# A gated recurrence on one core: each gate of each half in a PSUM bank of its own and turned by itself

## The chip, the cores and the metric

One core of one Trainium2 chip. The metric is the device time of one launch in microseconds; three runs of the kernel before took 1808.76, 1807.4 and 1808.27, median 1808.27.

## The reference

x has shape (8, 512, 512): 8 sequences (B) of 512 steps (T) of 512 features. Weights and state are float32.

```
def step(h, x_t):
    fused = sigmoid(concat([x_t, h]) @ w_W + w_b)
    r, z = split(fused, 2)
    memory = x_t @ wx_W + wx_b + r * (h @ wh_W + wh_b)
    h_new = z * h + (1 - z) * tanh(memory)
    return h_new, h_new
out = x + all h_new
```

In the kernel r is the gate of the first half of `fused`, m the memory part, z the second half of `fused`. The 512 steps depend on each other through h.

## The kernel before, in words

The 512 features of h are four chunks of 128 (KC = 4), in two halves: A holds chunks 0 and 1, B chunks 2 and 3. For each step TensorE computes h @ [w_r, w_m, w_z] with h as the loaded weights (8 columns, the batch) and the weight matrix moving. Each product is split over four column tiles of 32 (`tile_position=(0, Q * j)`, j = 0 to 3), so the instructions go out in fours. A float32 matmul stands in the trace as two weight loads and two matmuls.

`products(group, half, s)` (line 226) makes the part of one group that comes from one half of h. The groups are RM_A (r and m of half A, 128 columns, bank 0), RM_B (bank 1), Z_A (64 columns, bank 2), Z_B (bank 3). `step` on TensorE (line 237): wait for half A of h, RM_A and RM_B of that half; wait for half B of h, RM_A, Z_A both halves, RM_B, wait until Z_B of the step before has been turned, Z_B both halves. Then `x_products` (line 214) makes 3 of the 48 chunk products of x for the block of 16 steps that comes next, from weights and x that SP loads anew (`wx_step`, `x_next`), into banks 4 to 6. TensorE's loop holds four steps, the other engines' 16.

VectorE turns a group (`turn`, line 322): a 32 by 32 block transpose from PSUM into `turned`, after which the features lie on partitions. Then it adds the x part (`sum_r` line 327, `sum_z` line 331), forms r * hm + xm in a scan (`mix_m`, line 335), and z * h - z * n + n in a scan (`mix_h`, line 343), which gives h. ScalarE makes the sigmoids (`reset` line 275, `update` line 279) and the tanh (`new` line 283), empties the x products (`empty`, line 264) and places them (`place_x`, line 271). GpSimd adds the bias to m (`hidden`, line 401) and x to the output (`add_x`, line 407).

The order on each engine is written out by hand in its `step` function (lines 237, 289, 351, 420). All waits are on counting semaphores. A wait is written ahead of the instruction it guards; where there are several, one rides on the instruction and the others are instructions of their own on the engine's queue. Each half of h has its semaphore `h_ready`, each group `..._done` (TensorE finished) and `..._turned` (VectorE finished).

Of the kernel before, what the change touches and what calls it, by code (L numbers as in the profile page):

```python
# [12 lines left out]
def build(nc, x, h0, w_h, w_x, b_x, b_h, out):  # L13
# [40 lines left out]
    with ctx:  # L54
# [30 lines left out]
        ps = ctx.enter_context(nc.psum_tensor("ps", [P, 8, 512], F32))  # L85
        X_BANK = 4

# [25 lines left out]

        rm_a_done = sem("rm_a_done")
        z_a_done = sem("z_a_done")
        rm_b_done = sem("rm_b_done")
        z_b_done = sem("z_b_done")
        rm_a_turned = sem("rm_a_turned")
        z_a_turned = sem("z_a_turned")
        rm_b_turned = sem("rm_b_turned")  # L120
        z_b_turned = sem("z_b_turned")
        x_product = sem("x_product")
# [9 lines left out]
        hm_ready = halves("hm_ready")  # L132
        xg_ready = sem("xg_ready")
        xg_turned = sem("xg_turned")
# [10 lines left out]
        def _(sp):  # L145
# [18 lines left out]

            for r in range(RING):
                load_wx(r)
                sp.dma_start(x_next[:, r], x_flat[:, :, TOK:2 * TOK]).then_inc(x_next_loaded[r], 16)  # L167
            sp.dma_start(x_sb[:, :, TOK:2 * TOK], x_flat[:, :, TOK:2 * TOK]).then_inc(x_loaded, 16)
            with sp.Fori(0, BLOCKS) as i:
# [4 lines left out]
                for s in range(STEPS):  # L174
                    if s % RING == 0:
                        turn = sp.snap(i * (STEPS // RING) + (s // RING + 1))
                    if s % RING < RING - 1:
                        sp.wait_ge(x_used[s % RING], turn)
                    else:
                        sp.wait_ge(x_product, sp.snap(i * UNITS + (s // RING + 1) * X_UNITS + UNITS))  # L180
                    load_wx((s + RING) % STEPS)
                    if s >= STEPS - RING:
                        sp.dma_start(x_next[:, s % RING], x_flat[:, :, cols]).then_inc(x_next_loaded[s % RING], 16)
                sp.wait_ge(y_added, sp.snap(i * STEPS + 2 * STEPS))
# [11 lines left out]
        def _(pe):  # L196
            def x_product_of(u, k, w, moving):
                for j in range(TILES):
                    at = slice(Q * j, Q * (j + 1))
                    mm = pe.matmul(ps[at, X_BANK + u % X_UNITS, 0:TOK], w[:, at], moving,  # L200
                                   start=(k == 0), stop=(k == KC - 1), tile_position=(0, Q * j))
                if k == KC - 1:
                    mm.then_inc(x_product, 1)
                return mm

            def first_x_products():
                for u, k in x_list:
                    if k == 0 and u >= X_UNITS:
                        pe.wait_ge(xg_ready, u - X_UNITS + 1)
# [4 lines left out]
            def x_products(i, s):  # L214
# [11 lines left out]
            def products(group, half, s):  # L226


                at, cols, bank = group
                for k in range(half * HC, (half + 1) * HC):  # L230
                    for j in range(TILES):
                        mm = pe.matmul(ps[Q * j:Q * j + B, bank, 0:cols], h_of(s - 1, k),  # L232
                                       wh[:, k, j, at:at + cols], start=(k == 0), stop=(k == KC - 1),
                                       tile_position=(0, Q * j))
                return mm

            def step(t0, s):
# [12 lines left out]

            pe.wait_ge(x0_loaded, 16)
            first_x_products()
# [3 lines left out]
            with nc.Fori(0, T // RING, engines=(mybir.EngineType.PE,), hint_back_edge=True) as i:  # L256
                t0 = pe.snap(i * RING)
                for s in range(RING):
                    step(t0, s)
                    x_products(i, s)  # L260

        @block.scalar
        def _(act):
            def empty(u, which, unit0):
                act.wait_ge(bias_loaded, 2 * 16)
                act.wait_ge(x_product, unit0 + (u + 1))
                dst = xg[:, which, :, u, :].rearrange("p a t b -> p (a t) b")
                act.activation(dst, ps[:, X_BANK + u % X_UNITS, 0:TOK].rearrange("p (t b) -> p t b", b=B),  # L268
                               ACT.Identity, bias=bias_x[:, u:u + 1]).then_inc(xg_ready, 1)

# [17 lines left out]

            def step(t0, s, this, other, unit0):
                nxt = held(act, t0 + (s + 1))  # L290
                reset(0, nxt)
                update(0, nxt)
                new(0, s, nxt)
                reset(1, nxt)
                update(1, nxt)
                new(1, s, nxt)
                for u in X_ENDS[s]:
# [3 lines left out]
                else:  # L301
                    act.wait_ge(xg_ready, unit0 + UNITS)
                    act.sem_inc(xg_turned, 1)
                    place_x(other, 0)
# [3 lines left out]
            for u in range(UNITS):  # L308
                empty(u, slice(0, 1), 0)
            act.wait_ge(xg_ready, UNITS)  # L310
            place_x(slice(0, 1), 0)
            with nc.Fori(0, BLOCKS, engines=(mybir.EngineType.Activation,), hint_back_edge=True) as i:
# [4 lines left out]
                for s in range(STEPS):  # L317
                    step(t0, s, this, other, unit0)

        @block.vector  # L320
        def _(dve):
            def turn(bank, o, g0, g1):
                cols = (g1 - g0) * HC * Q
                return dve.transpose(turned[:, o, g0:g1].rearrange("p g c q -> p (g c) q"),  # L324
                                     ps[:, bank, 0:cols].rearrange("p (c q) -> p c q", q=Q))

# [23 lines left out]

            def step(t0, i, s):
# [24 lines left out]
                mix_h(1, s, nxt)  # L376

            dve.sem_inc(z_b_turned, 1)
            dve.memset(ps[:, 0:GROUP_BANKS, :], 0.0).then_inc(ps_cleared, 1)  # L379
# [14 lines left out]
            with nc.Fori(0, BLOCKS, engines=(mybir.EngineType.DVE,), hint_back_edge=True) as i:  # L394
                t0 = dve.snap(i * STEPS)
                for s in range(STEPS):
                    step(t0, i, s)

        @block.gpsimd
        def _(pool):  # L400
            def hidden(o, par, nxt):
                pool.wait_ge(rm_b_turned if o else rm_a_turned, nxt)
                pool.tensor_tensor(add[:, par, o, M, :, 0].rearrange("p (c b) -> p c b", b=B), product_of(o, M),  # L403
# [79 lines left out]
```

## Time and profile before

| | |
|---|---|
| median of the runs | 1808.27 us |
| the profiled execution: its own time / span | 1807.97 / 1806.1 us |
| granted TensorE clock | 0.998 |
| TensorE busy, weight loads busy | 1787.5 us (99%), 1629.9 us (90%) |
| VectorE, ScalarE, GpSimd busy | 1160.5 us (64%), 824.9 us (46%), 357.1 us (20%) |
| instructions on TensorE | 78208 matmuls, 78208 weight loads |
| DMA engines, mean busy share of the one hardware queue | 29.6% |
| weights `wx_step`: issue to landing | 2.4 us, 516 transfers of 192 KB |
| `x_next`: issue to landing | 3.2 us, 132 transfers of 256 KB |

Busy times are sums of the recorded durations; a matmul's end is modelled and matmuls overlap. PEld is the weight load of TensorE, DVE is VectorE, ACT ScalarE, POOL GpSimd, SP the queue that issues the DMAs. "idle before" is the time in which the engine stood still just before the instructions of a group, with what ended it.

### The profile page before, as it was taken

Reading aid. Unit: us, or ns where it says so; the run is one execution under the profiler, and the core shown is the slowest. Engines: PE = TensorE matmul, PEld = TensorE weight load, DVE = VectorE, ACT = ScalarE, POOL = GpSimd, SP = SyncE. Lnnn points to the kernel's source line nnn. Section 1 sums busy time; section 2 is a strip of 40 time slices with the busy share of each in tenths; the row PEclk is TensorE's granted clock in tenths of the full one; section 3 lists DMA queues with packets and bytes.
Section 4 is the critical chain, followed back from the end, with each engine's and each line's share of the span. In section 5 each row is a group of like instructions: output and inputs, shape, how many; then the busy total and the mean of one; then the engine's idle time right before and its main releaser. Section 6 shows DMA issues by size and latency. Waiting matters only on the chain.

```text
span 1806.1 us, 178513 instructions
## 1 busy us (share of the span) xinstructions
PE 1787.5 (99%) x78208; PEld 1629.9 (90%) x78208; DVE 1160.5 (64%) x6153; ACT 824.9 (46%) x3983; POOL 357.1 (20%) x1540
## 2 busy tenths in 40 slices
PE   7999999999999999999999999999999999999998
PEld 6999999999999999999999999999999999999997
DVE  2666666666666666666666666666666666666665
ACT  2444444444444444444444444444444444444444
POOL 0222222222222222222222222222222222222221
PEclk9999999999999999999999999999999999999999
DMA  6222333223332223332233322233322333223332
GB/s 218 87 67 86 91 91 91 73 75 91 91 91 85 69 86 92 92 92 69 81 92 92 91 77 74 88 91 91 91 68 80 91 91 92 74 74 94 92 92 82
DMA packets 180731, 159.86 MB, mean 89 GB/s; under 512 B 12016, under 2 KB 179440, under 8 KB 180720
## 3 DMA queue, kind: packets, MB, share of 16 engines
q1 hardware_dynamic: 180720, 159.72, 29.6%
q8 instruction: 7, 0.11, 0.0%
q14 instruction: 4, 0.03, 0.0%
HBM read 151.28 MB, written 8.39 MB: 88 GB/s over the span
## 4 chain that ended last, share of the span: by engine, by line
PE 98%; SPq 1%; DMA 0%; issue 0%; DVE 0%; ACT 0%; POOL 0%; POOLq 0%; DVEq 0%
PE ps L232 78%; PE ps L200 20%; SPq L167 0%; SPq L162 0%; DMA x_sb<-in_x 0%; SPq L153 0%; SPq L159 0%; DVE turned L324 0%; SPq L150 0%; DVE h L347 0%; DVE m_pre L338 0%; SPq L157 0%; SPq L156 0%; SPq L155 0%; DVE pre_r L328 0%
## 5 line engine op out<-in xcount | busy, mean ns | idle before, releaser
L232 PE MATMUL ps<-wh,h 128*8 128x128 f32 (+1 forms) x65536 | 1504.7, 246 | 2.6 <-issue 2.2
L232 PEld LDWEIGHTS ps<-wh,h 128*8 128x8 f32 x65536 | 1324.7, 90 | 143.1 <-DVE h L347 113.5
L324 DVE STREAM_TRANSPOSE turned<-ps 128x128 f32<-128x128 f32 (+1 forms) x2048 | 550.4, 269 | 412.4 <-PE ps L232 412.4
L277 ACT ACTIVATE m_by<-pre_r 128x16 f32<-128x16 f32 x1024 | 224.2, 219 | 701.2 <-DVE pre_r L328 701.2
L200 PE MATMUL ps<-x_next,wx_step 128*32 128x128 f32 x12288 | 433.0, 274 | 0.6 <-issue 0.6
L347 DVE TENSOR_TENSOR_SCAN h<-h_by,h 128x48 f32<-128x48 f32 x1024 | 274.2, 268 | 152.4 <-ACT h L286 152.4
L403 POOL TENSOR_TENSOR add<-turned,bias_h 128x16 f32<-128x16 f32 x1024 | 222.8, 218 | 709.9 <-DVE turned L324 681.5
L281 ACT ACTIVATE h_by<-pre_z 128x16 f32<-128x16 f32 x1024 | 229.6, 224 | 249.8 <-DVE pre_z L332 246.0
L200 PEld LDWEIGHTS ps<-x_next,wx_step 128*32 128x32 f32 x12288 | 316.1, 110 | 16.2 <-issue 4.3
L416 POOL TENSOR_TENSOR y<-x_sb,h 128x32 f32 x512 | 134.0, 262 | 734.5 <-DVE h L347 734.5
L286 ACT ACTIVATE h<-m_pre 128x32 f32<-128x32 f32 x1024 | 237.8, 232 | 1.8 <-DVE m_pre L338 1.8
L338 DVE TENSOR_TENSOR_SCAN m_pre<-m_by,add 128x32 f32<-128x32 f32 x1024 | 223.2, 218 | 1.8 <-POOL add L403 1.8
L332 DVE TENSOR_TENSOR pre_z<-turned,add 128x16 f32<-128x16 f32 x1024 | 180.3, 176 | 35.0
L328 DVE TENSOR_TENSOR pre_r<-turned,add 128x16 f32<-128x16 f32 x1024 | 179.8, 176 | 34.9
L268 ACT ACTIVATE xg<-ps,bias_x 128x128 f32 (+1 forms) x396 | 145.6, 368 | 15.0 <-PE ps L200 14.9
L273 ACT ACTIVATE add<-xg 128x96 f32 (+1 forms) x513 | 145.6, 284 | 3.9
L200 PE MATMUL ps<-x_sb,wx 128*32 128x128 f32 x384 | 15.1, 323 | 9.8 <-DMA wx<-in_w_x 6.1
L200 PEld LDWEIGHTS ps<-x_sb,wx 128*32 128x32 f32 x384 | 13.3, 131 | 11.0 <-issue 10.3
L379 DVE MEMSET ps<- 128x2048 f32 x1 | 1.8, 1765 | 1.3 <-PEq L475 1.3
L391 DVE COPY h<-h 128x8 f32<-128x8 f32 x4 | 0.4, 170 | 2.9 <-DMA h<-in_h 2.9
L307 ACT ACTIVATE warm<-bias_h 128x4 f32<-128x4 f32 x1 | 0.2, 205 | 4.3 <-DMA bias_h<-in_b_h 4.3
L307 ACT ACT_TABLE_LOAD x1 | 1.3, 1283 | 0.7 <-PEq L475 0.7
(8 smaller groups left out, 1.1 us busy)
## 6 DMA issues: line engine op xcount, KB each, us to landing
wx_step<-in_w_x SPq DMA_DIRECT2D x516, 192.0 KB, 2.4
x_next<-in_x SPq DMA_DIRECT2D x132, 256.0 KB, 3.2
x_sb<-in_x SPq DMA_DIRECT2D x34, 256.0 KB, 3.2
out_h<-y SPq DMA_DIRECT2D x32, 256.0 KB, 2.9
wx<-in_w_x SPq DMA_DIRECT2D x6, 512.0 KB, 7.3
wh<-in_w_h SPq DMA_DIRECT2D x4, 768.0 KB, 11.0
bias_x<-in_b_x SPq DMA_DIRECT2D x1, 6.0 KB, 3.2
bias_h<-in_b_h SPq DMA_DIRECT2D x1, 2.0 KB, 3.6
```

The source lines that it names most:

```text
L200: mm = pe.matmul(ps[at, X_BANK + u % X_UNITS, 0:TOK], w[:, at], moving, start=(k == 0), stop=(k == KC - 1), tile_position=(0, Q * j))
L232: mm = pe.matmul(ps[Q * j:Q * j + B, bank, 0:cols], h_of(s - 1, k), wh[:, k, j, at:at + cols], start=(k == 0), stop=(k == KC - 1), tile_po ...
L268: act.activation(dst, ps[:, X_BANK + u % X_UNITS, 0:TOK].rearrange("p (t b) -> p t b", b=B), ACT.Identity, bias=bias_x[:, u:u + 1]).then_i ...
L277: act.activation(m_by[:, o, :, 1], pre_r[:, o, :], ACT.Sigmoid).then_inc(r_ready[o], 1)
L281: act.activation(h_by[:, o, :, 2], pre_z[:, o, :], ACT.Sigmoid).then_inc(z_ready[o], 1)
L286: act.activation(n_twice, m_pre[:, o, :, 1].unsqueeze(2).to_broadcast([P, HB, 2]), ACT.Tanh)\
L324: return dve.transpose(turned[:, o, g0:g1].rearrange("p g c q -> p (g c) q"), ps[:, bank, 0:cols].rearrange("p (c q) -> p c q", q=Q))
L328: dve.tensor_tensor(pre_r[:, o].rearrange("p (c b) -> p c b", b=B), product_of(o, R), x_of(par, o, R), ALU.add).then_inc(r_summed[o], 1)
L332: dve.tensor_tensor(pre_z[:, o].rearrange("p (c b) -> p c b", b=B), product_of(o, Z), x_of(par, o, Z), ALU.add).then_inc(z_summed[o], 1)
L338: dve.tensor_tensor_scan(m_pre[:, o].rearrange("p i w -> p (i w)"), m_by[:, o].rearrange("p i w -> p (i w)"), add[:, par, o, M].rearrange( ...
L347: dve.tensor_tensor_scan(h[:, s % RING, o, 0:REGION], h_by[:, o].rearrange("p i w -> p (i w)"), h[:, (s - 1) % RING, o, 1:1 + REGION], 0.0 ...
L403: pool.tensor_tensor(add[:, par, o, M, :, 0].rearrange("p (c b) -> p c b", b=B), product_of(o, M), bias_h[:, HC * o:HC * (o + 1)].unsqueez ...
```

## The change

- Six groups instead of four: r, m and z of each half, 64 columns each, in banks 0 to 5 (`GATES * o + g`); the host lays the columns of w_h out to match. Each has its own `done` and `turned` semaphore and its own turn on VectorE: six turns of 64 columns per step instead of two of 128 and two of 64.
- TensorE's order: half A of h for r0, m0, z0 and m1; wait for half B of h; r0, m0, z0 (second half), r1 whole, m1 (second half), z1 whole. The wait for Z_B's turn is gone.
- VectorE's order: turn r0, turn m0, sum r0, turn z0, turn r1, sum z0, mix_m 0, turn m1, sum r1, mix_h 0, turn z1, mix_m 1, sum z1, mix_h 1.
- ScalarE's order: the tanh of half B comes ahead of the sigmoid of its z.
- The x products use banks 6, 7, 6 for units 0, 1, 2, with a semaphore for each of the three in place of one. TensorE no longer waits for `x_next`: SP waits for it before it issues the weights. The values TensorE waits for are computed once per loop pass, between the groups.
- At the start SP issues the four `x_next` loads first, then waits for each before its `wx_step` load.

```
-    RM_A = (0, P, 0)
-    RM_B = (P, P, 1)
-    Z_A = (2 * P, P // 2, 2)
-    Z_B = (2 * P + P // 2, P // 2, 3)
-    GROUP_BANKS = 4
+    GROUP = HC * Q
+    GROUP_BANKS = HALVES * GATES
+    X_BANKS = [GROUP_BANKS, GROUP_BANKS + 1, GROUP_BANKS]
...
@@ sync: start, and steps 12 to 15 of a block
             for r in range(RING):
+                sp.dma_start(x_next[:, r], x_flat[:, :, TOK:2 * TOK]).then_inc(x_next_loaded[r], 16)
+            for r in range(RING):
+                sp.wait_ge(x_next_loaded[r], 16)
                 load_wx(r)
-                sp.dma_start(x_next[:, r], x_flat[:, :, TOK:2 * TOK]).then_inc(x_next_loaded[r], 16)
...
+                    if s >= STEPS - RING:
+                        sp.dma_start(x_next[:, s % RING], x_flat[:, :, cols]).then_inc(x_next_loaded[s % RING], 16)
+                        sp.wait_ge(x_next_loaded[s % RING], sp.snap(i * 16 + 32))
                     load_wx((s + RING) % STEPS)
...
@@ tensor: x products
-                pe.wait_ge(wx_step_loaded[s], held(pe, i * 16 + 16))
-                pe.wait_ge(x_next_loaded[s], held(pe, (i // (STEPS // RING)) * 16 + 16))
+                pe.wait_ge(wx_step_loaded[s], loaded)
...
-                        pe.wait_ge(xg_ready, held(pe, i * X_UNITS + (UNITS - X_UNITS + u + 1)))
+                        if u == 0:
+                            pe.wait_ge(xg_free[2], free)
+                        elif u == 1:
+                            pe.wait_ge(xg_free[1], free)
+                        else:
+                            pe.wait_ge(xg_free[0], again)
...
@@ tensor: one step
                 pe.wait_ge(h_ready[0], nxt)
-                products(RM_A, 0, s)
-                products(RM_B, 0, s)
+                products(0, R, 0, s, True)
+                products(0, M, 0, s, True)
+                products(0, Z, 0, s, True)
+                products(1, M, 0, s, True)
                 pe.wait_ge(h_ready[1], nxt)
-                products(RM_A, 1, s).then_inc(rm_a_done, 1)
-                products(Z_A, 0, s)
-                products(Z_A, 1, s).then_inc(z_a_done, 1)
-                products(RM_B, 1, s).then_inc(rm_b_done, 1)
-                pe.wait_ge(z_b_turned, nxt)
-                products(Z_B, 0, s)
-                products(Z_B, 1, s).then_inc(z_b_done, 1)
+                products(0, R, 1, s, False).then_inc(r_done[0], 1)
+                products(0, M, 1, s, False).then_inc(m_done[0], 1)
+                products(0, Z, 1, s, False).then_inc(z_done[0], 1)
+                products(1, R, 0, s, True)
+                products(1, R, 1, s, False).then_inc(r_done[1], 1)
+                products(1, M, 1, s, False).then_inc(m_done[1], 1)
+                products(1, Z, 0, s, True)
+                products(1, Z, 1, s, False).then_inc(z_done[1], 1)
...
@@ scalar: one step
                 reset(1, nxt)
+                new(1, s, nxt)
                 update(1, nxt)
-                new(1, s, nxt)
...
@@ vector: one step
+                dve.wait_ge(r_done[0], nxt)
                 if s % RING == 0:
                     dve.wait_ge(y_added, held(dve, t0 + (s + STEPS)))
-                dve.wait_ge(rm_a_done, nxt)
-                turn(0, 0, R, Z).then_inc(rm_a_turned, 1)
-                dve.wait_ge(rm_a_turned, nxt)
+                turn(0, R).then_inc(r_turned[0], 1)
+                dve.wait_ge(m_done[0], nxt)
+                turn(0, M).then_inc(m_turned[0], 1)
                 dve.wait_ge(x_placed, nxt)
+                dve.wait_ge(r_turned[0], nxt)
                 sum_r(0, par, nxt)
-                dve.wait_ge(z_a_done, nxt)
-                turn(2, 0, Z, GATES).then_inc(z_a_turned, 1)
-                dve.wait_ge(z_a_turned, nxt)
+                dve.wait_ge(z_done[0], nxt)
+                turn(0, Z).then_inc(z_turned[0], 1)
+                dve.wait_ge(r_done[1], nxt)
+                turn(1, R).then_inc(r_turned[1], 1)
+                dve.wait_ge(z_turned[0], nxt)
                 sum_z(0, par, nxt)
                 mix_m(0, par, nxt)
-                dve.wait_ge(rm_b_done, nxt)
-                turn(1, 1, R, Z).then_inc(rm_b_turned, 1)
-                dve.wait_ge(rm_b_turned, nxt)
+                dve.wait_ge(m_done[1], nxt)
+                turn(1, M).then_inc(m_turned[1], 1)
+                dve.wait_ge(r_turned[1], nxt)
                 sum_r(1, par, nxt)
                 mix_h(0, s, nxt)
-                dve.wait_ge(z_b_done, nxt)
-                turn(3, 1, Z, GATES).then_inc(z_b_turned, 1)
-                dve.wait_ge(z_b_turned, held(dve, t0 + (s + 2)))
+                dve.wait_ge(z_done[1], nxt)
+                turn(1, Z).then_inc(z_turned[1], 1)
+                mix_m(1, par, nxt)
+                dve.wait_ge(z_turned[1], nxt)
                 sum_z(1, par, nxt)
-                mix_m(1, par, nxt)
                 mix_h(1, s, nxt)
```

## Rows read from the trace of the kernel before

**Rows 1.** The page: chain that ended last by engine; the queue that fetches code

```profile
PE 98%; SPq 1%; DMA 0%; issue 0%; DVE 0%; ACT 0%; POOL 0%; POOLq 0%; DVEq 0%
...
q8 instruction: 7, 0.11, 0.0%
```

**Rows 2.** Groups of instructions, 300 to 1700 us: busy us, mean ns | idle before <-releasers

```profile
L232 PEld LDWEIGHTS ps<-wh,h 128*8 128x8 f32 x51824 | 1046.9, 90 | 110.1 <-DVE h L347 89.4
L232 PE MATMUL ps<-wh,h 128*8 128x128 f32 x25908 | 901.5, 273 | 0.0
L232 PE MATMUL ps<-wh,h 128*8 128x64 f32 x25920 | 510.4, 219 | 0.0
...
L200 PEld LDWEIGHTS ps<-x_next,wx_step 128*32 128x32 f32 x9720 | 249.8, 110 | 12.1 <-issue 3.2
...
L324 DVE STREAM_TRANSPOSE turned<-ps 128x64 f32<-128x64 f32 x810 | 188.9, 233 | 0.0
```

**Rows 3.** Chain of waits, 912 to 920 us: start us, us, what

```profile
914.45 0.66 PE ps L200 x24
```

**Rows 4.** Timeline of one step: start us, us, engine line op out<-in xcount [idle <-releaser]

```profile
912.49 0.34 PEld L232 LDWEIGHTS ps<-wh,h 128*8 128x8 f32 x16 [0.24 <-DVE h L347]
913.19 0.32 DVE L324 STREAM_TRANSPOSE turned<-ps 128x128 f32<-128x128 f32 x1 [0.75 <-PE ps L232]
...
913.64 0.25 DVE L324 STREAM_TRANSPOSE turned<-ps 128x64 f32<-128x64 f32 x1
...
913.92 0.18 DVE L332 TENSOR_TENSOR pre_z<-turned,add 128x16 f32<-128x16 f32 x1
914.01 0.22 DVE L338 TENSOR_TENSOR_SCAN m_pre<-m_by,add 128x32 f32<-128x32 f32 x1
...
914.15 0.29 DVE L324 STREAM_TRANSPOSE turned<-ps 128x128 f32<-128x128 f32 x1
...
914.47 0.18 DVE L328 TENSOR_TENSOR pre_r<-turned,add 128x16 f32<-128x16 f32 x1
...
914.57 0.28 DVE L347 TENSOR_TENSOR_SCAN h<-h_by,h 128x48 f32<-128x48 f32 x1
...
914.77 0.22 DVE L324 STREAM_TRANSPOSE turned<-ps 128x64 f32<-128x64 f32 x1
...
915.02 0.17 DVE L332 TENSOR_TENSOR pre_z<-turned,add 128x16 f32<-128x16 f32 x1
915.11 0.22 DVE L338 TENSOR_TENSOR_SCAN m_pre<-m_by,add 128x32 f32<-128x32 f32 x1
...
915.23 0.22 ACT L281 ACTIVATE h_by<-pre_z 128x16 f32<-128x16 f32 x1 [0.33 <-DVE pre_z L332]
915.36 0.23 ACT L286 ACTIVATE h<-m_pre 128x32 f32<-128x32 f32 x1
...
915.63 0.26 DVE L347 TENSOR_TENSOR_SCAN h<-h_by,h 128x48 f32<-128x48 f32 x1 [0.30 <-ACT h L286]
...
915.94 0.23 PEld L232 LDWEIGHTS ps<-wh,h 128*8 128x8 f32 x12 [0.22 <-DVE h L347]
```

**Rows 5.** Timeline, start of a step with s = 0 mod 4 (PEld, DVE)

```profile
902.10 1.22 PEld L232 LDWEIGHTS ps<-wh,h 128*8 128x8 f32 x64 [0.21 <-DVE h L347]
...
902.87 0.32 DVE L324 STREAM_TRANSPOSE turned<-ps 128x128 f32<-128x128 f32 x1 [0.82 <-PE ps L232]
```

**Rows 6.** Line 356, whole run: ns min/median/max, first and last start us

```profile
L356 DVEq EVENT_SEMAPHORE  x96: 21/21/21, 44.9 to 1788.2; - x96
```

**Rows 7.** Waits of the DMA queue, 800 to 1000 us: total us, times, longest us

```profile
SPq L162 <- PE ps L200: 157.7, 54, 3.2
```

**Rows 8.** Timeline of PE in the loop's first pass, first and last of four

```profile
32.25 1.24 PE L232 MATMUL ps<-wh,h 128*8 128x64 f32 x60 [0.28 <-issue]
...
42.71 0.63 PE L200 MATMUL ps<-x_next,wx_step 128*32 128x128 f32 x11 [0.59 <-issue]
```

**Rows 9.** DMA queues, 0 to 60 us: packets, MB, share of 16 engines

```profile
q8 instruction: 7, 0.11, 0.8%
```

More of the change, by code:

```diff
@@ L132, in build @@
         hm_ready = halves("hm_ready")
-        xg_ready = sem("xg_ready")
+        xg_free = [sem(f"xg_free{u}") for u in range(X_UNITS)]
         xg_turned = sem("xg_turned")
@@ L207, in first_x_products @@
                 for u, k in x_list:
-                    if k == 0 and u >= X_UNITS:
-                        pe.wait_ge(xg_ready, u - X_UNITS + 1)
+                    if k == 0 and u >= X_UNITS - 1:
+                        last = max(v for v in range(u) if X_BANKS[v % X_UNITS] == X_BANKS[u % X_UNITS])
+                        pe.wait_ge(xg_free[last % X_UNITS], last // X_UNITS + 1)
                     if k == 0 and u * WX_PARTS % UNITS == 0:
@@ L212, in first_x_products, with x_products @@
                     x_product_of(u, k, wx[:, u, k, :], x_sb[:, k, 0:TOK])
-            def x_products(i, s):
-                pe.wait_ge(wx_step_loaded[s], held(pe, i * 16 + 16))
-                pe.wait_ge(x_next_loaded[s], held(pe, (i // (STEPS // RING)) * 16 + 16))
+            def x_products(loaded, free, again, s):
+                pe.wait_ge(wx_step_loaded[s], loaded)
                 for n in range(X_EACH):
@@ L224, in x_products, with products @@
                     last.then_inc(x_used[s], 1)
-            def products(group, half, s):
-                at, cols, bank = group
+            def products(o, g, half, s, start):
+                bank = GATES * o + g
+                at = GROUP * bank
                 for k in range(half * HC, (half + 1) * HC):
                     for j in range(TILES):
-                        mm = pe.matmul(ps[Q * j:Q * j + B, bank, 0:cols], h_of(s - 1, k),
-                                       wh[:, k, j, at:at + cols], start=(k == 0), stop=(k == KC - 1),
-                                       tile_position=(0, Q * j))
-                return mm
@@ L237, in step @@
-            def step(t0, s):
+                        mm = pe.matmul(ps[Q * j:Q * j + B, bank, 0:GROUP], h_of(s - 1, k),
+                                       wh[:, k, j, at:at + GROUP], start=(start and k % HC == 0),
+                                       stop=(not start and k % HC == HC - 1), tile_position=(0, Q * j))
+                return mm
+            def step(i, t0, s):
+                nonlocal loaded, free, again
                 nxt = held(pe, t0 + (s + 1))
                 pe.wait_ge(h_ready[0], nxt)
-                products(RM_A, 0, s)
-                products(RM_B, 0, s)
-                pe.wait_ge(h_ready[1], nxt)
-                products(RM_A, 1, s).then_inc(rm_a_done, 1)
-                products(Z_A, 0, s)
-                products(Z_A, 1, s).then_inc(z_a_done, 1)
-                products(RM_B, 1, s).then_inc(rm_b_done, 1)
-                pe.wait_ge(z_b_turned, nxt)
-                products(Z_B, 0, s)
-                products(Z_B, 1, s).then_inc(z_b_done, 1)
+                products(0, R, 0, s, True)
+                products(0, M, 0, s, True)
+                if s == 0:
+                    loaded = held(pe, i * 16 + 16)
+                products(0, Z, 0, s, True)
+                if s == 0:
+                    free = held(pe, i + UNITS // X_UNITS)
+                    again = held(pe, i + (UNITS // X_UNITS + 1))
+                products(1, M, 0, s, True)
+                pe.wait_ge(h_ready[1], nxt)
+                products(0, R, 1, s, False).then_inc(r_done[0], 1)
[6 more added lines that the diff above has]
+                products(1, Z, 1, s, False).then_inc(z_done[1], 1)
@@ L251, in _ @@
+            loaded = free = again = None
             pe.wait_ge(x0_loaded, 16)
@@ L258, in _ @@
                 for s in range(RING):
-                    step(t0, s)
-                    x_products(i, s)
+                    step(i, t0, s)
+                    x_products(loaded, free, again, s)
         @block.scalar
@@ L287, in new, with step @@
                     .then_inc(tanh_ready[o], 1)
-            def step(t0, s, this, other, unit0):
+            def step(i, t0, s, this, other, unit0):
                 nxt = held(act, t0 + (s + 1))
@@ L301, in step @@
                 else:
-                    act.wait_ge(xg_ready, unit0 + UNITS)
-                    act.sem_inc(xg_turned, 1)
+                    for p in range(X_UNITS):
+                        act.wait_ge(xg_free[p], held(act, i * (UNITS // X_UNITS) + 2 * (UNITS // X_UNITS)))
+                        act.sem_inc(xg_turned, 1)
                     place_x(other, 0)
@@ L309, in _ @@
                 empty(u, slice(0, 1), 0)
-            act.wait_ge(xg_ready, UNITS)
+            for p in range(X_UNITS):
+                act.wait_ge(xg_free[p], UNITS // X_UNITS)
             place_x(slice(0, 1), 0)
@@ L317, in _, with turn @@
                 for s in range(STEPS):
-                    step(t0, s, this, other, unit0)
+                    step(i, t0, s, this, other, unit0)
         @block.vector
         def _(dve):
[L322 to L325, printed above, removed]
+            def turn(o, g):
+                return dve.transpose(turned[:, o, g], ps[:, GATES * o + g, 0:GROUP].rearrange("p (c q) -> p c q", q=Q))
             def sum_r(o, par, nxt):
@@ L396, in _ @@
                 for s in range(STEPS):
-                    step(t0, i, s)
+                    step(t0, s)
         @block.gpsimd
@@ L462 @@
     to_h = rows_h.reshape(P, KC, 3, J, 2, KC // 2, Q).transpose(0, 1, 3, 2, 4, 5, 6)
[L463 to L464 removed]
+    h_cols = to_h.transpose(0, 1, 2, 4, 3, 5, 6).reshape(P, KC, J, 3 * P)
     arrays = {
```

30 lines of the change are left out of this document (12 added, 18 removed).

## The prediction

> **What bounds the kernel now.** I read the chain of waits first, and it misleads a little: it puts 98% of the span on TensorE [rows 1]. TensorE's ends are modelled and overlap, so "busy" does not say whether work or a wait sets a step. The groups of instructions over 1400 us do. 810 transposes of half a step's z are 405 steps, so a step takes 1400/405 = 3.457 us, and 512 steps are 1770 us of the profiled 1806.1 us span [rows 2]. The matmuls go out in fours, one for each column tile of 32. The 24 of an x product stage take 0.66 us [rows 3], so a four of 128 columns takes 0.110 us. A 64-column matmul is 273 - 219 = 54 ns shorter, so its four takes 0.056 us. A step has 22 fours of 128 (16 of r and m, 6 of x) and 16 of 64 (z). That makes 22 x 0.109 + 16 x 0.056 = 3.29 us of pure streaming (0.109 closes better than 0.110 over the step). So TensorE has a hole of 0.16 us in each step. The weight loads show where: they idle before a load that VectorE's h scan releases, 89.4 us over those 405 steps, 0.22 us each, most of it this hole [rows 2]. The kernel is bound by the recurrence, from one second-half h to the next, and not by TensorE's work.
>
> The timeline of one step shows that loop [rows 4]. In hundredths of a us, from the weight load that waits for the second half of h (912.49): turn of half A's r and m at 0.70, turn of half A's z at 1.15, pre_z 1.43, m_pre 1.52, turn of half B's r and m 1.66, pre_r 1.98, h scan of half A 2.08, turn of half B's z 2.28, pre_z 2.53, m_pre 2.62, tanh 2.87, h scan of half B 3.14, next load 3.45. From the first z turn on every item starts as soon as the one before lets it. Each turn that had to wait for TensorE starts 0.26 after its last four has streamed: 4 x 0.109 = 0.44 gives 0.70, and 8 x 0.056 more gives 1.15.
>
> **The change, part by part.** (1) r and m in groups of 64 columns: 16 fours of 0.109 become 32 of 0.056, +0.04 us of TensorE work per step. A step of pure work is then 48 x 0.056 + 0.66 + 0.01 = 3.36 us, still under 3.457, so this lies in the hole and costs nothing by itself.
>
> (2) The new loop. Times t count from that same weight load. VectorE's program now has turn r0, turn m0, sum r0, turn z0, then turn r1, and only behind it sum z0. Half A's r, m, z take 12 fours and half B's r 8: r1 is complete at 20 x 0.056 = 1.12, plus 0.26: turn r1 starts at t = 1.38. Turn z0 could be summed at about 0.97 + 0.28 = 1.25, yet sum z0 stands behind turn r1. No row shows an independent instruction behind a turn. The others let the next one in about 0.08 before their recorded end: sum 0.18 long, next after 0.09; m_pre 0.22 long, next after 0.14; h scan 0.28 long, next after 0.20 [rows 4]. So I take 0.25 - 0.08 = 0.17 for a turn that waited (z at 913.64), and 0.22 - 0.08 = 0.14 for one that did not (914.77). The bounds are 0.09 (a sum's) and the whole turn with its signal, 0.28 and 0.25. Then: sum z0 1.55, m_pre 1.64, tanh +0.25 = 1.89, h scan A +0.27 (tanh to scan in the old tail, 915.36 to 915.63) = 2.16. Turn m1 and sum r1 fit before it (1.64 + 0.14 + 0.14 + 0.09 = 2.01). Turn z1 is at 2.16 + 0.20 = 2.36, against 2.28 before: 0.08 later.
>
> (3) The tail. m_pre of half B no longer waits for the z turn: 2.36 + 0.14 = 2.50, tanh 2.75. ScalarE's order is now tanh before the z sigmoid. The sigmoid goes in 0.14 behind the tanh (that spacing: 915.23 to 915.36), at 2.89, which is later than sum z1 allows (2.63 + 0.21). It is ready 0.22 + 0.03 later, at 3.14. So the h scan now waits last for z and no longer for tanh.
>
> (4) What that wait costs. Where an instruction waits for two semaphores, the first named rides on it and the second is an instruction of its own ahead. One step in four shows its price when it is the last to come. There the turn of r and m also waits for y, and TensorE's signal is taken by such a separate wait (96 of them, line 356). The turn starts at 902.87 - 902.10 = 0.77 and not at 0.70 [rows 4 to 6]. So 0.07 is paid when the separate one comes last. mix_h names tanh first and z second, hence z rides separately: scan B at 3.14 + 0.07 = 3.21. Bounds 0 and 0.09. From scan to load 0.31 as now: 3.52.
>
> (5) The same rule takes the y wait out of the way in that one step in four (0.07/4 = 0.02 per step, now in the 3.457): its separate wait is now y's, long past. The turn, r0, would be off the path in any case.
>
> (6) Fewer waits at x products, no wait for half B's turned z, a separate semaphore for each bank: TensorE has some 0.16 us spare in each new step (3.52 - 3.36), so shorter issue there gives nothing. Before, these waits were hidden in the hole as well. The h of half A arrives at 2.16 + 0.31 = 2.47, and the x products end at 32 x 0.056 + 0.66 = 2.45. That is a stall of 0.02 to 0.05, inside the same spare.
>
> (7) SP: in steps 12 to 15 it waits for x_next to land before it issues the weights. It waits 157.7/54 = 2.9 us per step now [rows 7], and the buffers are needed three steps (over 10 us) later: nothing. At the start, x_next before wx_step moves the second x load by about a us either way: taken as 0, range 1.5 us.
>
> Sum: 3.52 unrounded is 3.515, so 3.515 - 3.457 = +0.058 us x 512 = +29.7 us. The profiled execution took 1807.97 us (span 1806.1 and 1.9 around it), 0.3 under the median of the runs, so no correction: 1837.7, forecast **1837 us**.
>
> Size of the unknowns on the loop: both turns at 0.09 and the separate wait free: 3.33, under TensorE's 3.36, so TensorE would rule. Both turns whole, and 0.05 for the first four of 64 columns after a stall (its spacing could stay that of a 128 four): 3.79.
>
> The Trainium skill, "VectorE: DVE Perf Modes", section "The DRAIN you can't avoid", says the next VectorE op does not start until the pipe is empty, and its rules ask to keep the number of ops low; that speaks against two more turns per step. The rows go against it here: sums 0.18 long are followed after 0.09 [rows 4]. By the rows the sum is the 3.52 above, by that rule it is rival C below.
>
> **Rivals.** A, faster: the tail is as short as its lower bounds and TensorE sets the step. For it: half B's z is complete on TensorE 8 fours of r and m and 16 of z (0.87 + 0.90 = 1.77, plus 0.26 = 2.03) after the load but turned at 2.28, so VectorE and not TensorE was late there; and m_pre now starts before z is turned. Against it: sum z0 behind turn r1, and the separate wait of 0.07. Step 3.36 to 3.40: -0.097 x 512 = -50, 1758 us; with 0.04 of holes -29, 1779 us. I take 1765. It decides if the loop falls under 3.40, so if the three unknowns together give back 0.12 or more.
>
> B, no change: the z signal is not paid extra (0.07 gone) and the rest stands. 3.448 against 3.457: -0.009 x 512, 1803 us, at the edge of what can be told. The loop exchanges one late item for another.
>
> C, a turn holds VectorE to its end: 0.11 more at each of turns r1 and z1, signal included, 3.74: +145, 1953 us; without the signal's share (0.08 each) 3.68, 1922 us. For it: no row shows a turn followed at once. Against it: every other op of this engine lets the next in early. This is what the drain rule of the Trainium skill, cited above, would make of the turns.
>
> D, code: TensorE's loop grows from 4 x 304 = 1216 to 4 x 432 = 1728 matmuls and weight loads. The whole run now fetches 7 packets of code [rows 1], all in its first 60 us, with four issue waits of 0.28 to 0.59 in the loop's first pass [rows 8, 9]; later passes fetch none, so the loop stays loaded. If the longer one does not, seven fetches of 0.45 per four steps cost 0.79 a step, about +400: 2210 us. The Trainium skill, "Runtime: NRT & Kernel Launch", section "Instruction fetch mechanics", gives TensorE room for 2048 instructions, which would hold 1728; the same section's remark on two cache lines would not, and the 7 packets disagree with it already for the present loop.
>
> **How the numbers follow.** Forecast 0.50 (its own range 1815 to 1865), A 0.24, B 0.14, C 0.06, D 0.06. A change of under 0.2% (1804.7 to 1811.9 us) can't be told from none; of B I count 0.05 as faster and 0.09 as the same. Faster 0.24 + 0.05 = 0.29, same 0.09, slower 0.50 + 0.06 + 0.06 = 0.62. The range 1775 to 1890 leaves out about half of A, C and D: some 0.2.
>
> **What would show it.** After: the turn of r1 starts 1.38 after the load that waits for h; sum z0 0.17 behind it; h scan of half B released last by the z sigmoid and not by tanh; step 3.51 to 3.52; the idle time of TensorE's weight loads still near 0.2 us per step, now in two places. The prediction is wrong if that idle time is near none (A), if a sum follows a turn after 0.22 or more (C), or if code packets exceed about 12 (D).

## The result, and the profile after

The changed kernel took 1795.56 us (median of 4 runs, 1794.16 to 1796.07), the kernel before 1808.51 beside it: ratio 0.9927, 95% interval 0.991 to 0.9944. It is 13 us faster; the forecast was 29 us slower. The profiled execution has a span of 1793.5 us.

Two things moved, in opposite directions. The step is the mean distance of the same signal over 360 steps of one profiled execution; the rest is the span of that execution less 512 such steps, so it holds the start of the run and also its end. Each ratio is to runs of the kernel before made beside that kernel.

| kernel | step, us | rest, us | median, us | ratio to before (95%) |
|---|---|---|---|---|
| before | 3.458 | 35.4 | 1808.51 | |
| after | 3.415 | 45.3 | 1795.56 | 0.9927 (0.991 to 0.9944) |
| e1: sum z0 ahead | 3.344 | 45.5 | 1759.73 | 0.9727 (0.971 to 0.9743) |
| e2: z rides | 3.353 | 43.2 | 1768.16 | 0.9774 (0.9758 to 0.9791) |
| e3: x early | 3.415 | 45.7 | 1795.98 | 0.9925 (0.9909 to 0.9942) |
| e4: x waits back | 3.427 | 45.7 | 1801.95 | 0.9956 (0.994 to 0.9973) |
| e5: tail back | 3.472 | 44.7 | 1824.28 | 1.0082 (1.0065 to 1.0099) |
| e6: y wait back | 3.417 | 46.0 | 1797.45 | 0.993 (0.9914 to 0.9947) |
| e7: sum waits | 3.567 | 43.9 | 1872.25 | 1.0344 (1.0327 to 1.0361) |
| b1: before, tail order | 3.468 | 36.7 | 1814.45 | 1.0025 (1.0016 to 1.0035) |
| b2: before, 64 columns | 3.469 | 44.2 | 1822.27 | 1.0068 (1.0051 to 1.0085) |
| v2: half B joined | 3.362 | 44.9 | 1766.82 | 0.9761 (0.9745 to 0.9777) |
| v3: joined, turned apart | 3.335 | 43.7 | 1753.05 | 0.9681 (0.9665 to 0.9698) |

The steps brought (3.458 - 3.415) x 512 = -22 us, the rest took 9.9 us back. The rest spreads from 43.2 to 46.0 us over the changed kernel and e1 to e7, one execution each, so a difference of 1 or 2 us in it can't be told from none. The profiled execution of e2 took 1762.96 us, 5 us under the median of its four runs (1762.96 to 1770.16): its step and rest belong to a faster execution than its median.

Of the 9.9 us, 2.7 lie at the end: from the start of the last h scan to the end of the span it is 1806.1 - 1800.98 = 5.2 us before and 1793.5 - 1785.60 = 7.9 us after. The last rows of SP and GpSimd show why, first before:

```profile
1801.52 0.26 POOL L416 TENSOR_TENSOR y<-x_sb,h 128x32 f32 x1 [1.43 <-DVE h L347]
1802.09 0.64 SPq L186 DMA_DIRECT2D out_h<-y  x1
```

then after:

```profile
1785.95 0.55 SPq L181 DMA_DIRECT2D x_next<-in_x  x1
1786.13 0.26 POOL L437 TENSOR_TENSOR y<-x_sb,h 128x32 f32 x1 [1.38 <-DVE h L365]
1789.18 0.33 SPq L158 DMA_DIRECT2D wx_step<-in_w_x  x1
1789.85 0.64 SPq L186 DMA_DIRECT2D out_h<-y  x1
```

SP now waits until x_next has landed before it issues the weights, and the last store of the output stands behind both on its queue. It is issued 3.7 us after the last addition of x starts, and 0.6 us after it in the kernel before. The same holds in all ten kernels with the new wait (3.3 to 4.0 us) and in none of the three without it (0.6 us). No run took this wait out by itself. The other 7 us lie ahead of the last h scan; b2 and e3 below show where.

The groups of the kernel after, 300 to 1700 us, beside [rows 2] (busy us, mean ns | idle before). The idle time in front of the weight loads is 54.8 us over 410 steps, 0.13 us each, where it was 0.27:

```profile
L239 PE MATMUL ps<-wh,h 128*8 128x64 f32 x78739 | 1202.5, 219 | 0.0
L239 PEld LDWEIGHTS ps<-wh,h 128*8 128x8 f32 x78729 | 1111.6, 90 | 54.8 <-DVE h L365 0.2
```

The timeline of VectorE and ScalarE after, from the turn of r1 on, which answers to [rows 4]:

```profile
916.57 0.25 DVE L343 STREAM_TRANSPOSE turned<-ps 128x64 f32<-128x64 f32 x1 [0.20 <-PE ps L239]
916.74 0.14 DVE L350 TENSOR_TENSOR pre_z<-turned,add 128x16 f32<-128x16 f32 x1
916.80 0.21 DVE L356 TENSOR_TENSOR_SCAN m_pre<-m_by,add 128x32 f32<-128x32 f32 x1
...
917.04 0.23 ACT L304 ACTIVATE h<-m_pre 128x32 f32<-128x32 f32 x1
917.07 0.14 DVE L346 TENSOR_TENSOR pre_r<-turned,add 128x16 f32<-128x16 f32 x1
...
917.31 0.26 DVE L365 TENSOR_TENSOR_SCAN h<-h_by,h 128x48 f32<-128x48 f32 x1
917.48 0.22 DVE L343 STREAM_TRANSPOSE turned<-ps 128x64 f32<-128x64 f32 x1
...
917.63 0.18 DVE L356 TENSOR_TENSOR_SCAN m_pre<-m_by,add 128x32 f32<-128x32 f32 x1
...
917.74 0.18 DVE L350 TENSOR_TENSOR pre_z<-turned,add 128x16 f32<-128x16 f32 x1
917.85 0.23 ACT L304 ACTIVATE h<-m_pre 128x32 f32<-128x32 f32 x1 [0.39 <-DVE m_pre L356]
917.98 0.21 ACT L299 ACTIVATE h_by<-pre_z 128x16 f32<-128x16 f32 x1
...
918.29 0.26 DVE L365 TENSOR_TENSOR_SCAN h<-h_by,h 128x48 f32<-128x48 f32 x1 [0.38 <-ACT h_by L299]
```

The order of events is the one forecast: turn r1 releases the chain, tanh comes ahead of the sigmoid, and the last scan is released by the sigmoid of z (`<-ACT h_by`), not by tanh. But see the durations: the sum at 916.74 is 0.14 long where every sum of [rows 4] is 0.17 or 0.18, and the m_pre scan at 917.63 is 0.18 long where it was 0.22. Both stand right behind a turn and wait for no signal that is still to come. The h scan of half A (917.31) is 0.26 long where it was 0.28 in [rows 4]; that one goes the other way, for it stood ready behind a sum there and waits for tanh here.

### The profile page after: what moved, and what is told of

Same layout as the page of the kernel before. It is cut to its first block, busy times and chain, and to the rows that moved or that the text cites. A ratio compares the mean times of both kernels' runs of the same rounds, so it can differ in the third digit from the quotient of the medians.

```text
span 1793.5 us, 244402 instructions
## 1 busy us (share of the span) xinstructions
PE 1766.1 (98%) x110976; PEld 1694.7 (94%) x110976; DVE 1131.5 (63%) x7177; ACT 789.8 (44%) x3983; POOL 357.1 (20%) x1540
## 4 chain that ended last, share of the span: by engine, by line
PE 97%; DMA 1%; SPq 1%; issue 0%; DVE 0%; ACT 0%; POOL 0%; POOLq 0%; DVEq 0%
PE ps L239 79%; PE ps L200 19%; DMA x_next<-in_x 1%; DMA x_sb<-in_x 0%; SPq L149 0%; SPq L158 0%; SPq L155 0%; DVE h L365 0%; SPq L146 0%; ACT h L304 0%; ACT h_by L299 0%; SPq L162 0%; SPq L153 0%; SPq L152 0%; SPq L151 0%
## 5 line engine op out<-in xcount | busy, mean ns | idle before, releaser
L239 PE MATMUL ps<-wh,h 128*8 128x64 f32 x98304 | 1504.4, 219 | 9.0 <-issue 5.1
L239 PEld LDWEIGHTS ps<-wh,h 128*8 128x8 f32 x98304 | 1390.9, 90 | 78.7 <-issue 6.7
L343 DVE STREAM_TRANSPOSE turned<-ps 128x64 f32<-128x64 f32 x3072 | 705.3, 239 | 402.6 <-PE ps L239 309.1
L365 DVE TENSOR_TENSOR_SCAN h<-h_by,h 128x48 f32<-128x48 f32 x1024 | 264.0, 258 | 245.0 <-ACT h_by L299 192.1
L299 ACT ACTIVATE h_by<-pre_z 128x16 f32<-128x16 f32 x1024 | 222.4, 217 | 220.6 <-DVE pre_z L350 220.6
L356 DVE TENSOR_TENSOR_SCAN m_pre<-m_by,add 128x32 f32<-128x32 f32 x1024 | 203.1, 198 | 3.6 <-POOL add L424 3.6
L350 DVE TENSOR_TENSOR pre_z<-turned,add 128x16 f32<-128x16 f32 x1024 | 158.8, 155 | 0.0
L346 DVE TENSOR_TENSOR pre_r<-turned,add 128x16 f32<-128x16 f32 x1024 | 142.5, 139 | 0.0
```

What stands on the lines that cost most here:

```text
L239: mm = pe.matmul(ps[Q * j:Q * j + B, bank, 0:GROUP], h_of(s - 1, k), wh[:, k, j, at:at + GROUP], start=(start and k % HC == 0), stop=(not ...
L299: act.activation(h_by[:, o, :, 2], pre_z[:, o, :], ACT.Sigmoid).then_inc(z_ready[o], 1)
L343: return dve.transpose(turned[:, o, g], ps[:, GATES * o + g, 0:GROUP].rearrange("p (c q) -> p c q", q=Q))
L350: dve.tensor_tensor(pre_z[:, o].rearrange("p (c b) -> p c b", b=B), product_of(o, Z), x_of(par, o, Z), ALU.add).then_inc(z_summed[o], 1)
L356: dve.tensor_tensor_scan(m_pre[:, o].rearrange("p i w -> p (i w)"), m_by[:, o].rearrange("p i w -> p (i w)"), add[:, par, o, M].rearrange( ...
L365: dve.tensor_tensor_scan(h[:, s % RING, o, 0:REGION], h_by[:, o].rearrange("p i w -> p (i w)"), h[:, (s - 1) % RING, o, 1:1 + REGION], 0.0 ...
```

## The experiments

**e1: sum z0 ahead of turn r1.** Is the recurrence still what sets the step?

```
                 turn(0, Z).then_inc(z_turned[0], 1)
-                dve.wait_ge(r_done[1], nxt)
-                turn(1, R).then_inc(r_turned[1], 1)
                 dve.wait_ge(z_turned[0], nxt)
                 sum_z(0, par, nxt)
                 mix_m(0, par, nxt)
+                dve.wait_ge(r_done[1], nxt)
+                turn(1, R).then_inc(r_turned[1], 1)
```

> The changed kernel with one edit on VectorE: sum z0 and mix_m 0 stand ahead of the turn of r1. Theory L (the recurrence loop still sets the step at 3.414 us, and sum z0 queued behind turn r1 is on it): the h of half A is ready 0.3 us earlier, the loop falls to about 3.2 us, below TensorE's work of 3.351, and TensorE takes over: step 3.36 to 3.37, so -0.05 x 512 = -25 us against the changed kernel, 1771 us. Theory P (TensorE's work already sets the step, the hole of 0.07 at the wait for half B being mere start-up): no change, 1795. The idle time of the weight loads in front of the wait for half B should be gone under L.

1759.73 us, 36 us under the changed kernel, more than the 25 expected: the step fell to 3.344, which is the bare streaming of 48 fours of 64 and 6 of 128 columns (3.335 in three steps of four in the trace) and 0.035 more in the step at the loop's branch, 0.009 on the mean. My 3.351 for TensorE's work was 0.007 too long. The groups, 300 to 1700 us (1636 more loads than after, the idle time down from 54.8 us):

```profile
L239 PEld LDWEIGHTS ps<-wh,h 128*8 128x8 f32 x80365 | 1158.7, 90 | 11.6 <-issue 2.3
```

So in the changed kernel the loop of waits still ruled, by 0.07 us a step, and the sum behind turn r1 was on it.

**e2: z rides.** Does a separate wait that comes last cost something?

```
-                dve.wait_ge(tanh_ready[o], nxt)
-                dve.wait_ge(z_ready[o], nxt)
+                first, second = (z_ready, tanh_ready) if o else (tanh_ready, z_ready)
+                dve.wait_ge(first[o], nxt)
+                dve.wait_ge(second[o], nxt)
```

> The changed kernel with one edit: in mix_h of half B the wait for z is named first (rides on the scan), the wait for tanh second. If a separate wait that comes last costs 0.063 us (scan 4153 - 4090 ns in the trace after), the loop falls from 3.414 to 3.35 and TensorE's 3.351 plus its gaps takes over: step 3.36 to 3.37, about -22 us, 1773 us. If the 0.063 is not a price of the separate wait but of the scan: no change, 1795.

1768.16 us, -27 by the medians (32 by the step of its faster profiled execution). From z sigmoid to scan it is 0.24 in its timeline, against 918.29 - 917.98 = 0.31 after:

```profile
917.29 0.21 ACT L299 ACTIVATE h_by<-pre_z 128x16 f32<-128x16 f32 x1
917.53 0.26 DVE L366 TENSOR_TENSOR_SCAN h<-h_by,h 128x48 f32<-128x48 f32 x1 [0.31 <-ACT h_by L299]
```

The wait's price, read before from the y wait [rows 4 to 6], is confirmed: the scan starts 0.07 sooner. TensorE's work (3.344) all but takes over at 3.353.

**e7: the sum waits.** Is an op behind a turn really done sooner when it waits for nothing?

```
+                dve.wait_ge(r_turned[1], nxt)
                 dve.wait_ge(z_turned[0], nxt)
                 sum_z(0, par, nxt)
```

> The changed kernel with one wait more: sum z0 also waits until the turn of r1 right ahead of it has ended (it doesn't need its data), named first so that it rides. Theory Q (an op queued behind a running op of the same engine without a wait has 0.04 of its fixed part hidden, an op that waits for a signal has not): sum z0 starts 0.284 after the turn instead of 0.173 and m_pre ends 0.312 instead of 0.268 after it: +0.155 per step, +79 us, 1875 us. Rival (the sum's shorter record, 0.133 for 0.176, is an artefact of the record and the result comes no earlier): +0.111 per step, +57 us, 1853 us.

1872.25 us, step 3.567, +0.152. Its turn r1, sum z0 and m_pre:

```profile
915.66 0.25 DVE L343 STREAM_TRANSPOSE turned<-ps 128x64 f32<-128x64 f32 x1 [0.20 <-PE ps L239]
915.94 0.18 DVE L350 TENSOR_TENSOR pre_z<-turned,add 128x16 f32<-128x16 f32 x1
916.03 0.22 DVE L356 TENSOR_TENSOR_SCAN m_pre<-m_by,add 128x32 f32<-128x32 f32 x1
```

From the sum's start to the end of m_pre it is 0.09 + 0.22 = 0.31 here and 0.06 + 0.21 = 0.27 in the changed kernel. The later start of the sum alone (0.28 behind the turn for 0.17) makes 0.11 of the 0.152; the other 0.04 is this, so it is real time and not a matter of the record.

**e5: the tail's order back.**

```
                 reset(1, nxt)
-                new(1, s, nxt)
                 update(1, nxt)
+                new(1, s, nxt)
...
-                mix_m(1, par, nxt)
                 dve.wait_ge(z_turned[1], nxt)
                 sum_z(1, par, nxt)
+                mix_m(1, par, nxt)
```

> The changed kernel with the tail's order as before: sum z ahead of mix_m for half B on VectorE, the z sigmoid ahead of the tanh on ScalarE. From turn to next load: sum z 0.25 after the turn, m_pre 0.09, tanh 0.25, scan 0.26, load 0.31: 1.17 instead of 1.124: +0.044 per step, +22 us, 1817 us, if the tail's order carries the gain. If m_pre queued behind the sum is also 0.04 shorter than in the kernel before (as ops behind a turn are), +0.01 per step, 1800 us.

1824.28 us, +29: step +0.057. In its trace m_pre, again behind the sum, takes 0.251 from its start to tanh's, where the changed kernel takes 0.215. The tail's order carries more than the whole gain of the steps (0.043); without it the change would be a loss.

**b1: the tail's order alone, in the kernel before.** The same reordering of VectorE and ScalarE, the other way round.

> The kernel before with the tail's order alone changed: mix_m of half B ahead of sum z, tanh ahead of the z sigmoid on ScalarE. Theory L: the tail from turn to next load takes 1.124 us as in the changed kernel instead of 1.170, step 3.458 - 0.045 = 3.413, -23 us, 1785 us. Rival: the gain of the changed kernel comes from the split of r and m (r ready sooner) and the tail order alone loses, since z now comes last by a separate wait: +0 to +0.02 per step, 1808 to 1818 us.

1814.45 us, +5 beside its own before (ratio 1.0025): the rival. Its timeline shows one part of it:

```profile
917.33 0.17 DVE L328 TENSOR_TENSOR pre_r<-turned,add 128x16 f32<-128x16 f32 x1
...
917.62 0.22 DVE L324 STREAM_TRANSPOSE turned<-ps 128x64 f32<-128x64 f32 x1
917.79 0.23 DVE L338 TENSOR_TENSOR_SCAN m_pre<-m_by,add 128x32 f32<-128x32 f32 x1
```

m_pre needs r's sigmoid, 0.46 after pre_r (917.33 to 917.79), and the joined turn leaves only 0.29 between pre_r and the z turn. After, it is 917.48 - 917.07 = 0.41. So m_pre waits and is 0.23 long for 0.18. The other part is the one that the expectation named: z now comes last, by a separate wait (0.07). As the waits are named here, the order pays only where r is turned early; neither edit gains alone. The same order in the kernel before with z's wait named first was not run.

**b2: the kernel before with 64-column products.** `products` issues each 128-column group as two of 64, in the same bank; nothing else.

```
                 for k in range(half * HC, (half + 1) * HC):
+                    for c0 in range(0, cols, P // 2):
...
-                        mm = pe.matmul(ps[Q * j:Q * j + B, bank, 0:cols], h_of(s - 1, k),
+                            mm = pe.matmul(ps[Q * j:Q * j + B, bank, c0:c0 + P // 2], h_of(s - 1, k),
```

> The kernel before, with r and m of a half still in one bank and turned together, but issued as two 64-column products instead of one of 128. TensorE's work grows from 3.294 to 3.34 us per step and its loop from 1216 to 1728 matmuls and weight loads, nothing else changes. Theory L: the work lies in the hole; only the part on the loop counts (8 fours of 0.056 for 4 of 0.109, 0.01 us per step, +5 us), and the start grows by 8 to 10 us because the code of the first pass is fetched in pieces of 16 KB about every 3.8 us and there are two pieces more: 1822 to 1825 us in all. Rival 1: the start of the changed kernel was not the code: start as before, 1813. Rival 2: TensorE's extra work counts in full: +21 us from the steps alone.

1822.27 us: step 3.469 (+0.011) and rest 44.2 (+8.8), both as expected. TensorE's extra 0.04 of work lay in the hole. SP's order is that of the kernel before here, and all but 0.7 of the 8.8 us lie ahead of the last h scan: they are the price of the longer code.

**e3: x early.** The second x_sb load goes ahead of the x_next loads.

```
+            sp.dma_start(x_sb[:, :, TOK:2 * TOK], x_flat[:, :, TOK:2 * TOK]).then_inc(x_loaded, 16)
             for r in range(RING):
                 sp.dma_start(x_next[:, r], x_flat[:, :, TOK:2 * TOK]).then_inc(x_next_loaded[r], 16)
...
-            sp.dma_start(x_sb[:, :, TOK:2 * TOK], x_flat[:, :, TOK:2 * TOK]).then_inc(x_loaded, 16)
```

> The changed kernel with one edit at the start: the second load of x_sb is issued ahead of the x_next loads. The start of the changed kernel is 9.8 us longer than before (span less 512 steps: 45.2 against 35.4). If that comes from GpSimd waiting for x_sb until 30.7 us (28.6 before), with the TensorE pause and the lower clock after it: 6 to 9 us less, 1787 to 1790 us. If it comes from the code fetches of the longer loop: at most 2 us less. The step stays 3.414.

1795.98 us, rest 45.7: nothing. In the kernel after, GpSimd did stand until x_sb came (first row below). In e3 that wait is gone, and code takes its place in the chain of waits (rows below it; start us, us, what):

```profile
30.97 0.22 POOL L424 TENSOR_TENSOR add<-turned,bias_h 128x16 f32<-128x16 f32 x1 [30.53 <-DMA x_sb<-in_x]
```

```profile
36.79 1.59 issue
...
40.36 1.77 issue
...
44.42 1.78 issue
```

The code queue of the whole run has 9 packets, 7 before [rows 1]:

```profile
q8 instruction: 9, 0.15, 0.0%
```

The granted clock does not explain the rest either. At the start it stands at its lower level (1.2 GHz) in one stretch before, in b2 and in e3, in two after, and in none in e2 and e5, whose rest is 43.2 and 44.7 all the same.

**e4: the x products' waits back.** `x_products` again waits for x_next too and computes its values in place.

> The changed kernel with the waits at the x products as in the kernel before: TensorE also waits for x_next, and the values it waits for are computed in place. The gap before x products of step 0 mod 4 was 0.127 + 0.019 us before and is 0 to 0.01 now; the hole at the wait for half B is 0.07 in the changed kernel. Theory L: about 0.07 of the 0.146 shows once in four steps, +0.018 per step, +9 us, 1805 us. If the waits are fully hidden, 1795; if they count in full, +0.036 per step, +19 us.

1801.95 us, step +0.013: two thirds of what was expected if part is hidden. "Fewer waits at x products" is worth 6 us now. As I read it, the hole that hid them has shrunk to 0.07.

**e6: the y wait named first again.**

> The changed kernel with the wait for y named first again, so that in one step of four TensorE's r0 signal is the separate wait and turn r0 starts 0.06 later. Theory L: turn r0 is off the loop (turn r1 sets it): no change, 1796 us. Rival: it counts as in the kernel before: 0.06/4 per step, +8 us, 1804 us.

1797.45 us, step +0.002: no change that counts.

**v2 and v3: a version from the findings.** Both take e1's and e2's edits and make r and m of half B one product of 128 columns again, its first half ahead of the wait for half B. v2 turns it at once, v3 as r and then m.

```
+                cols = 2 * GROUP if (o, g) == (1, R) else GROUP
...
-                products(1, M, 0, s, True)
+                products(1, R, 0, s, True)
                 pe.wait_ge(h_ready[1], nxt)
...
-                products(1, R, 0, s, True)
                 products(1, R, 1, s, False).then_inc(r_done[1], 1)
-                products(1, M, 1, s, False).then_inc(m_done[1], 1)
```

> A version from the findings: e1's order and e2's wait order, and r and m of half B again as one group of 128 columns, made ahead of the wait for half B and turned together; half A stays split. With e1 TensorE sets the step at 3.344 us, so its work now counts in full: 8 fours of 0.109 replace 16 of 0.056, 3.316 us plus 0.009 at the loop's branch, -0.02 x 512 = -10 us, and one code piece less at the start, -2 to -4 us: 1745 to 1749 us. Rival: turning half B's r and m together brings the recurrence back over TensorE's work: above 1760 us.

1766.82 us: the rival. The long turn and a sum that must wait for it delay the h scan of half A, and TensorE stands 0.037 in front of half A's h. The h scan stands ready behind the sum again, and is 0.28 long again.

```profile
916.51 0.29 DVE L343 STREAM_TRANSPOSE turned<-ps 128x128 f32<-128x128 f32 x1
...
916.84 0.18 DVE L348 TENSOR_TENSOR pre_r<-turned,add 128x16 f32<-128x16 f32 x1
...
916.93 0.28 DVE L368 TENSOR_TENSOR_SCAN h<-h_by,h 128x48 f32<-128x48 f32 x1
```

> The last version with half B's r and m still one product of 128 columns in one bank, but turned as r and then m, 64 columns each, both behind the product. In the last version the h scan of half A came 0.036 after its tanh allowed it, behind the long turn and the sum that waited for it, and TensorE stood 0.037 per step in front of the h of half A. If that was the cause, TensorE's work of 3.316 us sets the step with at most 0.02 of holes: 3.32 to 3.335, 512 x -0.033 = -14 to -20 us against 1766.8: 1746 to 1752 us, below e1's 1759.7. Rival: the h of half A stays late because half B's r is only complete with its m: 1760 us or more.

1753.05 us, 0.9681 of before (0.9665 to 0.9698): step 3.335. One microsecond above the range expected in time, at the upper end of it in the step, and the fastest of all. In its timeline the two turns stand as one row of 0.35, the sum 0.28 behind their start instead of 0.33, and the scan waits for tanh alone (914.68 + 0.27):

```profile
914.57 0.35 DVE L343 STREAM_TRANSPOSE turned<-ps 128x64 f32<-128x64 f32 x2
914.68 0.24 ACT L303 ACTIVATE h<-m_pre 128x32 f32<-128x32 f32 x1
914.85 0.16 DVE L346 TENSOR_TENSOR pre_r<-turned,add 128x16 f32<-128x16 f32 x1
914.95 0.26 DVE L366 TENSOR_TENSOR_SCAN h<-h_by,h 128x48 f32<-128x48 f32 x1
```

The joined product also makes the loop shorter, 1472 instructions of TensorE, and the code queue has one packet less:

```profile
q8 instruction: 8, 0.13, 0.0%
```

That was expected to give 2 to 4 us. The rest is 44.9 (v2) and 43.7 (v3) against 45.5 in e1: 0.6 and 1.8 us, no more than the spread above. In both, GpSimd stands for x_sb as in the kernel after; in v2 this ends at 32.3 us, and TensorE then comes out of a wait of 4.9 us for h:

```profile
32.27 0.22 POOL L425 TENSOR_TENSOR add<-turned,bias_h 128x16 f32<-128x16 f32 x1 [31.82 <-DMA x_sb<-in_x]
```

Neither was run with x_sb early.

## Why the prediction was wrong

- **What bounds the kernel** was right: TensorE had a hole, the recurrence set the step. b2 (0.04 more work for +0.011) and e1 show it for both kernels.
- **(1)** TensorE's extra work lies in the hole: right for the step (b2). What was left out is that 1728 instructions instead of 1216 must be fetched once: +8.8 us in b2. Rival D saw the code but looked only for fetches in later passes; there are none.
- **(2), turn to sum.** Turn r1 at 1.38 after the load, sum z0 0.17 behind it: both measured (0.173). The sum's place behind turn r1 is on the loop (e1).
- **(2) and (3), the failed terms.** I gave every op the length and the spacing that it has in the rows of before. Three links of the loop come about in another way there. Sum z0 stands ready behind a turn now, where it had waited for its own turn's signal: sum to m_pre took 0.053 for 0.094. m_pre of half B stands ready behind a turn, where it had stood behind a sum: m_pre to tanh took 0.215 for 0.251. The h scan of half A waits for tanh, where it had stood ready behind a sum: scan to turn z1 took 0.174 for 0.202. That is 0.105 together. The other links differ by 0.005 in all, and the loop is 3.415 for the forecast 3.515, 51 us over 512 steps. Each of the three comes back when an edit brings the old situation back: the sum in e7, m_pre in e5, the h scan in v2. Why an op is shorter or longer by what stands in front of it is open.
- **(3), the tail's order** was seen as a near wash: 0.85 from turn z1 to the scan for 0.86 before. It took 0.81, and e5 measures the order at 0.057. Most of the difference is the m_pre link above, and not another term. b1 shows that the order hangs on r turned early, which the prediction did not say.
- **(4)** 0.07 for a separate wait that comes last: right (e2).
- **(5)** That turn r0 is off the path was right (e6).
- **(6)** "Gives nothing" was right for a hole of 0.16 and wrong for the real one of 0.07: 6 us (e4).
- **(7), the second failed term.** The rest of the run was priced at 0 with a range of 1.5: it measured 9.9. Some 7 us are the first fetch of the longer code (b2). 2.7 us are SP's wait for x_next, which the prediction looked for in the steps, where none shows; it did not look at the end, where the last store of the output stands behind it. The swapped loads made x_sb come 2 us later, but in the kernel after that is in the shade of the code (e3).
- With both turns at 0.09 and the separate wait free, the terms give 3.515 - 0.08 - 0.05 - 0.07 = 3.32 and not 3.33. Nothing hangs on it.

With the two mis-sized terms, 1837.7 - 51 + 9.9 = 1796.6. That 1795.56 lies inside the range of 1775 to 1890 is luck: the two mis-sized terms have opposite signs. Rival B (1803) was nearest in time, but its mechanism, the z signal not paid extra, is refuted by e2. Rival A (TensorE rules) had the right sign, but its mechanism had not come about: it needed e1's or e2's edit. Rival C (a turn holds VectorE to its end) is refuted by the sum 0.17 behind a turn 0.25 long; here the measurement differs from the drain rule that the prediction cited from the Trainium skill, "VectorE: DVE Perf Modes". For D, the room for 2048 instructions that the Trainium skill, "Runtime: NRT & Kernel Launch", section "Instruction fetch mechanics", states agrees with a loop of 1728 that is fetched once.

Of the signs on record, the order of events, the 1.38, the 0.17 and the few packets of code (9) came true. The step of 3.51 to 3.52 did not, and the idle time of the weight loads is 0.13 a step for "near 0.2".

Open: why the fetch of the first pass takes about 3.8 us for each 16 KB piece was not tried. That it is the loop's code, and not where the loads stand, is shown for the kernel after; the shorter loops of v2 and v3 did not bring the 2 to 4 us expected.

## What to carry to other kernels

In a loop of signals between engines, an op's recorded length and the start of the next op depend on what stands in front of it and on whether it waited: take the price of a queued op from an op queued in the same way. Name first the wait that comes last, and let no op that is ready stand behind one that waits for another engine: those two edits of order gave 27 and 36 us, each by itself, where the whole restructuring gave 13. They do not add up, since either one brings the step to within 0.01 of TensorE's work. Count the instructions of a loop's first pass when a split adds some, and join what no latency needs apart. When a wait is put into a queue, look at what stands behind it in the last pass too: here it was the last store.

## What the runs showed of the hardware

- VectorE lets the next op in 0.15 behind the start of a turn (64 columns) that had not waited, and 0.17 when it had (kernel after). A sum or an m_pre scan that stands ready behind such a turn is recorded 0.04 shorter (0.14 for 0.18, 0.18 for 0.22), and e7 and e5 show that this time is real. The h scan goes the other way: ready behind a sum it is 0.28 long and the next op starts after 0.20 (before, v2); when it has waited for tanh it is 0.26 long and the next starts after 0.17 (after).
- A second wait, as an instruction of its own, costs 0.07 us when it comes last: the h scan of half B starts 0.10 us behind the recorded end of z's sigmoid in the kernel after and 0.03 behind it where z's wait rides (e2). Served early, it costs nothing that shows: tanh's wait is the separate one in e2.
- TensorE's code came in pieces of 0.15 MB / 9 = 16 KB, and none came in later passes of the loop; 512 more instructions in the loop cost 8.8 us in b2, 17 ns each. 256 fewer in v2 and v3 gave 0.6 and 1.8 us, so this is no price for every loop.
